# Writing the loops of a fused kernel out: four attentions and a two-expert stage without loop instructions, and late layer-norm scales spread over seven steps

## The reference

```python
x = x + L0_xattn(layernorm(x), ctx, ctx, mask)      # L0a: 16 heads of 8, softmax
x = x + L0_ffn(layernorm(x))                        # L0f: 8 soft experts
x = x + L1_xattn(ctx, layernorm(x), mask, ...)      # L1a: relative bias, key mask, softmax
x = x + L1_ffn(layernorm(x))                        # L1f: top 1 of two relu experts, and a shared one
x = x + L2_xattn(layernorm(x), ctx, ctx, mask)      # L2a: masked scores, no softmax
x = x + L2_ffn(layernorm(x))                        # L2f: top 1 of 7 swiglu experts, and a shared one
x = x + L3_xattn(layernorm(x), ctx, ctx, mask)      # L3a: one head of 128, then a norm
x = x + L3_ffn(layernorm(x))                        # L3f: attention whose projections are mixed per batch row
# inside one attention with heads
scores = einsum('bhqd,bhkd->bhqk', q, k) * scale + bias_or_mask
x_out  = (softmax(scores) @ v) @ W_o + b_o
```

## Time and profile before

| what | value |
|---|---|
| time, median of 3 runs | 2151.9 us (2150.73 to 2154.13) |
| profiled execution | 2150.0 us, span 2148.3 us, mean granted clock 0.923 |
| L0a | about 17 to 302 us |
| L1a | about 476 to 800 us |
| L1f | about 800 to 1102 us |
| L2a | about 1102 to 1296 us |
| L3f | about 1846 to 2148 us |

### The profile page before, as it was taken

One profiled execution on the slowest core, in us unless ns is written; L12 is line 12 of the kernel. 1 busy time (PEld: TensorE's weight loads), 2 busy tenths in 40 slices (PEclk: granted clock), 3 DMA queues, 4 the chain that ended last, 5 costly groups with the idle time before them and its releaser, 6 DMA issues. The chain is left out here.

```text
span 2148.3 us, 86799 instructions
## 1 busy us (share of the span) xinstructions
PE 1907.1 (89%) x32111; PEld 1451.7 (68%) x32111; DVE 1628.0 (76%) x3712; ACT 1364.7 (64%) x3729; POOL 1104.0 (51%) x1286
## 2 busy tenths in 40 slices
PE   5999987989999979999989995999993973799998
PEld 3777754767777758888867773887772431677776
DVE  6788877866777768888856667777664786699998
ACT  4677766655555545666645554667772753599997
POOL 5566632873333325555568882756775754233332
PEclk9999996999999989999999997999996555799999
DMA  5111111000000002000001110113442520000000
GB/s 123 46 47 48 48 40 39 21 6 18 14 14 15 14 27 87 1 0 0 0 21 35 35 30 16 47 61 110 139 142 76 145 70 22 2 17 15 15 15 21
DMA packets 174358, 87.98 MB, mean 41 GB/s; under 512 B 70892, under 2 KB 168840, under 8 KB 174216
## 3 DMA queue, kind: packets, MB, share of 16 engines
q1 hardware_dynamic: 163656, 63.36, 11.0%
q0 software_dynamic: 7296, 21.38, 3.4%
q10 hardware_dynamic: 3264, 1.38, 0.3%
HBM read 66.13 MB, written 19.93 MB: 40 GB/s over the span
## 5 line engine op out<-in xcount | busy, mean ns | idle before, releaser
L1494 POOL TENSOR_TENSOR L1f_hl<-L1f_h,L1f_hh 128x512 fp32r<-128x512 f32 x128 | 167.2, 1307 | 126.1 <-DVE L1f_hh L1506 125.8
L1455 ACT ACTIVATE L1f_h<-L1f_H,L1f_w_b 128x512 f32<-128x512 f32 x192 | 132.0, 688 | 104.9 <-PE L1f_H L925 98.0
L399 POOL TENSOR_TENSOR L1a_wide<-L1a_flat,head_of_row 128x512 f32<-128x512 f32 x64 | 66.6, 1040 | 200.6 <-ACT L1a_flat L597 158.3
L399 POOL TENSOR_TENSOR L3f_wide<-L3f_flat,head_of_row 128x512 f32<-128x512 f32 x64 | 66.7, 1042 | 189.9 <-PE L3f_S L469 167.6
L1506 DVE CAST L1f_hh<-L1f_h 128x512 fp32r<-128x512 f32 x192 | 127.8, 672 | 31.7 <-ACT L1f_h L1455 30.6
L625 DVE TENSOR_REDUCE L1a_mx<-L1a_S 128x16 f32<-128x1024 f32 x64 | 78.4, 1224 | 80.8 <-PE L1a_S L469 80.8
L1841 ACT ACTIVATE L2f_both_act<-L2f_both_A 128x512 f32<-128x512 f32 x114 | 68.2, 598 | 92.1 <-PE L2f_both_G L925 91.2
L1872 DVE TENSOR_TENSOR L2f_both_h<-L2f_both_G,L2f_both_act 128x512 f32<-128x512 f32 x114 | 78.2, 686 | 63.6 <-ACT L2f_both_act L1841 63.1
L399 POOL TENSOR_TENSOR L0a_wide<-L0a_flat,head_of_row 128x512 f32<-128x512 f32 x64 | 66.6, 1040 | 95.0 <-ACT L0a_xhat L610 90.1
L625 DVE TENSOR_REDUCE L0a_mx<-L0a_S 128x16 f32<-128x1024 f32 x64 | 78.3, 1224 | 31.1 <-PE L0a_S L469 31.0
L1778 POOL TENSOR_TENSOR L2f_both_hl<-L2f_both_h,L2f_both_hh 128x512 fp32r<-128x512 f32 x66 | 85.6, 1297 | 31.4 <-ACT L2f_both_hh L1846 26.6
(11 more groups left out here) (534 smaller groups left out, 6815.6 us busy)
## 6 DMA issues: line engine op xcount, KB each, us to landing
L0a_mask_raw<-mask SPq DMA_DIRECT2D x256, 32.0 KB, 1.8
sorted_x<-L1f_zero SPq DMA_DIRECT2D x4, 1408.0 KB, 12.3
L2f_both_xhat<-sorted_x SPq DMA_DIRECT2D x22, 256.0 KB, 3.9
sorted_y<-L2f_both_y_out SPq DMA_DIRECT2D x22, 256.0 KB, 3.9
L0a_ctxT<-ctx_T SPq DMA_DIRECT2D x64, 64.0 KB, 1.9
L1a_ctxT<-ctx_T SPq DMA_DIRECT2D x64, 64.0 KB
L1a_mask_raw<-mask SPq DMA_DIRECT2D x256, 0.1 KB
L2a_ctxT<-ctx_T SPq DMA_DIRECT2D x64, 64.0 KB
```

The lines of the kernel that those rows point to most:

```text
L399: pool.tensor_tensor(wide[:, s], flat[:, s, :].rearrange("p (b n) -> p b n", b=B2).unsqueeze(2).broadcast_to([P, B2, 4, S]), c.head_of_row ...
L1455: act.activation(h[:, q % 3, :], psH[:, q % 2, :], ACT.Relu, bias=b1[:, q:q + 1]).then_inc(h_kept, 1)
L1494: pool.tensor_tensor(hl[:, q % 3, :], h[:, q % 3, :], hh[:, q % 3, :], ALU.subtract).then_inc(hl_pool, 1)
```

## The change

`run_steps` writes all steps out. The loop instruction is gone for the four attentions and for L1f, on every engine. What had relied on a tile's number being a register in the middle is put in terms of the number: in L0a, ACT's wait for the late scales moves from the end of step 11 to the end of step 15, and the 17 instructions of step 8 are spread over steps 8 to 14 (four, two, two, two, two, two, three). In L2a, PE's waits that had stood in the head and the tail alone are cut to the tiles that need them.

```diff
 def run_steps(eng, count, depth, ring, step):
-    head = depth + ring
-    assert depth % ring == 0 and (count - head) % ring == 0 and count >= head
-    for i in range(head):
-        step(i, i % ring)
-    if count > head:
-        with eng.Fori(0, (count - head) // ring) as turn:
-            for r in range(ring):
-                step(turn * ring + (head + r), r)
-    for i in range(count, count + depth):
+    for i in range(count + depth):
         step(i, i % ring)
...
-                if ready and isinstance(i, int) and i == DEPTH + RING - 1:
+                if ready and i == ready - 1:
                     wait(act, rest_made, 1)
...
                         rest.moments(dve, 0, 0)
                         rest.between(dve, 0)
+                    if i == 9:
                         rest.total(dve, 0)
                         rest.variance(dve, 0)
+                    if i == 10:
                         rest.seed(dve, 0)
-                        for k in range(3):
-                            rest.squared(dve, 0, k)
-                            rest.scaled(dve, 0, k)
-                            rest.refined(dve, 0, 0, k)
+                        rest.squared(dve, 0, 0)
+                    if i == 11:
+                        rest.scaled(dve, 0, 0)
+                        rest.refined(dve, 0, 0, 0)
+                    if i == 12:
+                        rest.squared(dve, 0, 1)
+                        rest.scaled(dve, 0, 1)
+                    if i == 13:
+                        rest.refined(dve, 0, 0, 1)
+                        rest.squared(dve, 0, 2)
+                    if i == 14:
+                        rest.scaled(dve, 0, 2)
+                        rest.refined(dve, 0, 0, 2)
                         rest.shift(dve, 0, 0)
...
-                    if isinstance(u, int):
+                    if u == 1:
                         wait(pe, xT_kept, u)
...
-                    if isinstance(u, int):
-                        wait(pe, v_kept, u + 4, NT)
+                    if u >= NT - 4:
+                        wait(pe, v_kept, NT)
                     wait(pe, pv_kept, u + 1)
...
-                    if isinstance(u, int):
+                    if u >= NT - 3:
                         wait(pe, v_kept, u + 1)
-                        wait(pe, pv_kept, u)
```

## The result

The changed kernel takes 2136.5 us (median of 4 runs, 2135.11 to 2139.35). The kernel before, timed beside it, takes 2151.32 us (4 runs, 2149.88 to 2154.13). The ratio is 0.9929, 95% interval 0.9917 to 0.9941: 14.8 us less, where 10.1 was forecast.

A forecast was written before the change was run, and what follows sets the result against it. No looped stage has an idle engine: PE fills L0a, L1a and L2a, DVE and ACT fill L3f. Gains 6.3 + 4.2 + 2.3 + 3.8 + 0 - 6.5 = 10.1 us give 2141.8 us, range 2130 to 2149.

The forecast's parts named there:

- L1a: Loop of L1a written out: 52 steps at 4.697 us, 244.2 instead of 246.48, a gain of 2.3 us.
- L3f: Loop of L3f written out: 52 steps at 4.38 us, 227.8 instead of 231.61, a gain of 3.8 us.
- L1f: Loop of L1f written out: PE's products already follow without a gap, 17.89 us per group, gain 0.
- the step that failed: L2a's 52 steps written out were priced at 2.983 us each, 155.1 against 148.6: a loss of 6.5 us.
- the other bound: L2a's faster straight steps, 2.747 us each, 142.8 for 52 steps: a gain of 5.8 us.
- Rival B: L2a is fed instructions well enough, its stops belonging to the stage's start: gain 22.4 us, 2129.5 in all; chance 0.17.
- L0a's loop: Loop of L0a written out: 52 steps at 4.063 us, 211.3 instead of 215.45, a gain of 4.2 us.
- rival D: L0a pays for its instructions as L2a does, 16.3 us over 52 steps: 2158.1 us in all; chance 0.08.
- The tail at 4.063: Three written-out intervals at L0a's end, 4.063 us a step, taken as evidence that L0a's instructions arrive in time.
- The links: Late scales in L0a, spread over seven DVE steps: 7.8 us of delay less 1.5 lost, a gain of 6.3 us.
- rival C: Every L0a step's links meet POOL's L399, 0.8 us lost per step: gain 6.0 us, 2145.9 in all; chance 0.12.
- the forecast's own range: Whole kernel: 2137 to 2146 us around 2141.8, with chain 5 to 7.5 and L2a's loss 3 to 8; chance 0.58.

The follow-up runs named there:

- experiment 2: The changed kernel with all 17 instructions of the late scales back in one step of L0a (writing out alone): 2143.03 us, ratio 0.9955.
- experiment 5: The changed kernel with four long-met waits put into each L2a step on PE: 2259.13 us, on another chip where the kernel before takes 2250.66.
- experiment 6: The kernel before, L2a still a loop, with four long-met waits in each L2a step on PE: 2250.52 us against 2250.66.
- experiment 1: The kernel before, loops kept, with the late scales' links spread over steps 8 to 14 of L0a: 2150.9 us against 2152.21, ratio 0.9994.
- experiment 4: The changed kernel with the four PE waits that the change drops kept in every L2a step: 2150.68 us against 2152.21 for the kernel before.
- experiment 3: The changed kernel with each step's links put behind less_max instead of behind BatchNorm on DVE: 2135.2 us, ratio 0.9926.
- experiment 7: The changed kernel with two waits (v_kept, pv_kept) kept ahead of the 64 small products of each L2a step: 2253.2 us against 2250.66 before.
- experiment 8: The changed kernel with one long-met wait ahead of the 64 small products of each L2a step: 2141.84 us against 2151.38 before.
- experiment 9: The changed kernel with one long-met wait more ahead of the 16 score products of each L2a step: 2137.55 us against 2151.38 before.
- experiment 10: The changed kernel with 24 long-met waits more at the head of each L2a step on PE: 2214.68 us.
- experiment 11: The kernel before, L2a a loop, with 24 long-met waits more in each L2a step on PE: 2229.57 us.

## Why the prediction was right, and where it was wrong

1. **The method held.** Setting a written-out step beside a loop step in the same stage gave L1a (2.35 against 2.3), L3f (3.6 against 3.8) and L1f (0) to 0.2 us, and experiment 2 gave the same two again.

2. **L2a: the step that failed.** "I take 2.983 for all 52 steps of L2a", because it was "the row of code that had been streaming for some steps". The right value was the other bound: 144.99/52 = 2.788. Rival B's mechanics were right in this stage. The reading of the stops as PE waiting for instructions was right, and experiments 5 and 6 bear it out: the same waits cost 18 us in code that comes once and 0.3 in code that is repeated. What was wrong is one sentence further on: "in the 12 head steps a few PE waits go, which I cost at 0". These waits are what the four head steps paid for. Tiles 7 to 11 take 11.7 to 12.0 in every kernel that keeps the four waits there (before, experiments 1, 4, 6), and 10.97 or 10.98 in the changed kernel and in experiments 2 and 3. I had priced new code by rows of old code that differed in just the thing that the diff removes. The diff showed it; the price of a wait on an engine that is already full should have been asked. The Trainium skill (Runtime: NRT & Kernel Launch, Instruction fetch mechanics) calls the crossing of a block "mostly hidden". The trace of the changed kernel agrees (0.4 us of such waits in 52 steps, with 37 packets, and 2.3 us in all over 52 steps of its usual 2.744); that of experiment 4, with two instructions more per step and 37 packets too, does not (7.6 us, and 15.2 in all).

3. **L0a's loop: the mechanism of rival D, at a small size.** Forecast was a gain of 4.2. The written-out 52 steps are the same code in eight kernels with the same order of work, and take 213.20 (changed), 215.11, 214.49, 217.61, 218.63, 218.51, 214.77 and 217.25 (experiments 2, 4, 5, 7, 8, 9, 10), on average 216.2. The loop takes 214.90, 214.35, 214.96 and 214.81 (before, experiments 1, 6, 11), on average 214.8. So 213.20 is the best of eight, and over the eight writing out L0a gains nothing or loses some 1.4 us. In total it was no lucky execution of the changed kernel: its span of 2135.0 lies in the middle of the kernel's four (2133.4 to 2137.6). Nor do the places of PE's instructions tell the kernels apart, since experiments 2 and 3 edit DVE's stream alone and take 215.11 and 217.43. What does, no run shows. PE's waits over the 52 steps of experiment 8, whose steps are up to 5.02 us long:

```profile
PE L0a_S L454 <- issue: 1.1, 2, 0.7
PE L0a_O L504 <- issue: 0.6, 2, 0.3
PE L0a_S L461 <- issue: 0.5, 2, 0.3
```

These rows hold 2.2 of the 7.2 us that the 52 steps take above 4.063 each; the rest stands in matmul rows that are longer in the late steps. All six stops end 1.3 to 1.5 us after an instruction packet, as in L2a. The tail at 4.063, my reason against D, was three steps. Most steps do take 4.06, but 7 (changed kernel) to 20 (experiment 8) of 52 take more, up to 5.2, and tiles 16, 19, 48, 51 and 61 are late in all eight. Stages and pace agree with this: L0a has 59 records per us and L2a 65.7, and there PE is late at times; L1a at 48 has nearly all its steps at 4.70, and experiment 10 slowed L2a down and had no stop either.

4. **The links: rival C's mechanism at half its price.** The sum said that two links fit into the gap ahead of POOL's L399, with 1.5 us lost in seven steps. All seven met it. In step 10 BatchNorm starts at 57.66 and POOL at 57.91, so POOL starts 0.25 after BatchNorm, not the 0.70 that I took from step 8; the second link starts at 58.08. Five steps lost 0.41 to 0.45, the first and the last 0.9, the seven 3.9, so the gain was 4.4 instead of 6.3. Experiment 3 removed the meeting and got all 3.9 back in place, which settles that cause. C had 0.8 per step, because it counted the link's whole excess, and part of that lies in time in which DVE waited for PE anyway (0.17 to 0.26 ahead of the maximum in five of the seven steps of experiment 3).

5. **Sum.** Against the forecast: links -1.9, L0a -2.5, L3f -0.2, L2a's 52 steps +10.1, its head +1.0, start -1.1, so 5.4 more; less the 2.2 between the stretches this is the 3.2 seen in the profiled spans (13.3 against 10.1). The total came out near, 5.3 us under 2141.8 and 0.5 under the forecast's own range of 2137 to 2146, because one term of the wrong sign was set off in part by two that were too large. Rival B, right about L2a, missed by more (2129.5), since it had the same two terms. That part is luck.

6. **Open.** Why one waiting instruction per step moves L2a from 145 to 156 us, while the change from 181 to 182 is half a per cent in pace: its place ahead of the 64 smallest products, or where the packets' borders fall in the step. In experiment 4 the four stops shown return every 20.6 to 21.0 us, seven steps apart, at nearly the same product (19, 19, 20 and 20 of the 64 left). That fits packets: 37 in 52 steps are five in 7.0 steps, so after seven steps the border between two packets is back at nearly the same place. But no run moved a border by itself, and none took other transfers out of the packets' way. Open too is why the links alone gave only 1.3 us: 4.4 are seen in their stretch, and in the profiled execution 1.5 go ahead of it and about 4 later, in stages that were not touched.

## What to carry to other kernels

A step that is written out can be priced by written-out steps of the same stage, but only if they hold the same instructions as the new ones: compare them line by line with the diff first, waits included. On an engine that is full, a wait that is sure to be met is an instruction as soon as another wait stands at its place, and in code that runs once it can cost far more than in a loop; leave out those that an earlier wait has already covered. When an engine idles for no visible reason, set these times beside those of the instruction packets. A short instruction for a gap should be put by what runs on the neighbouring engine at that moment, and tried at another place of the same step before it is split further.

## What the hardware showed that I had not expected

- A DVE instruction of 0.2 us with two operands in SBUF, started while POOL's 1.04 us spreading runs, takes 0.74 to 1.02 us and ends 0.06 or 0.07 us behind it, in each of the seven steps; at another place of the same step it takes 0.20 to 0.23. The Trainium skill (SBUF — State Buffer, SBUF: two separate sides) describes an exclusive lock on ports that the two engines share, held for the whole instruction, for a DVE instruction with two SBUF inputs against a GpSimd instruction that reads SBUF. The trace agrees where POOL starts first. Where DVE starts first it shows no price for POOL: a link with two inputs in SBUF ran from 62.34 to 62.53, POOL started at 62.43 and took its 1.04 all the same. In step 10 the instruction before, started 0.04 ahead of POOL, took 0.17.
- In code that comes once, PE's stops end 1.2 to 1.6 us after an instruction packet has ended: all 19 in L2a of experiment 4, 22 of experiment 5, 12 of experiment 7, and the six in L0a of experiment 8.
- On TensorE two waits share an instruction, and 24 met waits make a step 1.2 us longer, 0.05 each, in the loop as in written-out code.
- One more waiting instruction per step of L2a: 0.22 us per step where the code comes once, while two more cost under 0.01 in the loop.
- The same code of L0a took between 213.2 and 218.6 us from one kernel to the next, while L1f stayed within 261.30 and 261.38.
